# Indirect gathers without a bounds check, with valid row numbers in the empty slots

## The chip, the core and the metric

One core of a Trainium2 chip runs one program: one layer of a graph network over 50,000 nodes and 25,000 edges. The metric is the time of one execution on the device in microseconds (us), as the median of several runs. The engines have their own instruction streams and meet at semaphores: TensorE (PE; PEld is its weight load), VectorE (DVE), ScalarE (ACT), GpSimd (POOL) and SyncE (SP), and 16 DMA engines move the data.

## What is computed

```python
h = relu(layernorm(x))                                  # x: 50000 x 128, f32
agg = segment_sum(edge_attr, src, num_segments=50000)   # edge_attr: 25000 x 128, src: random nodes
z = silu(concat([h, agg]) @ W1 + b1) @ W2 + b2          # W1: 256 x 256, W2: 256 x 128
out = x + layernorm(z) * gamma + beta + h
```

The edges come in no order that is of use to the sum: each edge's row has to reach the node that its `src` names.

## The kernel before

The nodes are cut into NB = 49 blocks of BLOCK = 1024 rows, a block into TILES = 8 tiles of 128 nodes: tile t of a block holds nodes 8p + t, p from 0 to 127. A half block (HALF = 4 tiles) is the unit of work; a block's halves are c = 0 and 1. There are NT = 392 tiles.

**First stage, a sort (to about 125 us).** For each tile a table of 128 slots is filled with the edges whose source node lies in the tile. DVE makes one-hot rows, PE counts with them and places two words per slot (`slot_word`): the edge's number and the node inside the tile. A tile has 64 edges on average, so about half of its slots stay empty: word 0 is 0 there. `slot_tables` (DVE) turns the words into two tables, first for the tiles of FIRST_BLOCKS = 3 blocks (24 columns), later, in DVE's step of block 0, for the other 368: `slot_edge`, the row of `edge_attr` for each slot, and `slot_node`, the node in the tile. To an empty slot's values `empty` = 131072 is added, so that its row number lies beyond the end of the table and its node number matches no node. `link` makes DVE wait for the instruction it wraps. If a tile had more edges than slots, `spilled` is 1, and the other branch of POOL (`spill`) is taken; with these inputs it isn't.

**Second stage, the blocks.** For each tile POOL copies one column of `slot_edge` into `gather_rows` (`name_row`, L459) and issues one indirect DMA (`gather`, L471) that brings 128 rows of 512 bytes of `edge_attr` to G, a ring of RING = 3 blocks. The copy for tile t + 1 stands ahead of the gather of tile t. The gather has `bounds_check=limit, oob_is_err=False`: a row number over the limit moves nothing, G keeps what it held (G is zeroed once at the start). POOL runs two blocks ahead of PE at most: it waits until the edge sum three blocks back is done (`agg_done`).

PE's order for a half: `turn_h` (L636, transposes of the normalised rows), `sum_edges` (L643: waits for the four gathers (`gathered`) and for the one-hot tiles HOT, made by DVE from `slot_node` (L902), then multiplies G by HOT; an empty slot has a zero row in HOT, so whatever finite number lies in G counts for nothing), `layer1` (L654 to L659) and `layer2` of the half before (L667, L671). ACT casts the results to `hi` (L541, L543), DVE takes the rest as `lo` (L911), ACT applies Silu, squares and Relu; DVE does the statistics (`powers`), the scaling and the sums. SP loads X four blocks ahead (L332) and stores the results (L339). Every engine has its loop over blocks written by `run_blocks`: a few blocks in straight code, then a loop of six blocks a turn, and the rest in straight code.

POOL also makes the constants at the start: iotas (`own_node` at L392), zeroed G, then signals `late_const`, which DVE and PE wait for after the sort.

Of the kernel before, what the change touches and what calls it, by code (L numbers as in the profile page):

```python
# [15 lines left out]
P = 128  # L16
# [106 lines left out]
def gnn_layer(nc, x, src, edge_attr, W1, b1, W2, b2, gamma, beta, out):  # L123
# [13 lines left out]
    assert EC % UNROLL == 0 and UNROLL % STREAMS == 0 and NT <= 512  # L137

    HEAD = 2

    GROUP = max(n for n in range(1, 129) if edges % n == 0)

    with ExitStack() as ctx:
        def sb(name, shape, dt):
            return ctx.enter_context(nc.sbuf_tensor(name, shape, dt))
# [50 lines left out]
        edge_f = sb("edge_f", [P, NT], F32)  # L196
        empty = sb("empty", [P, NT], F32)
        own_part = sb("own_part", [P, NT], F32)
        slot_edge = sb("slot_edge", [P, NT], U32)
        slot_node = sb("slot_node", [P, NT], F32)  # L200
        spilled = sb("spilled", [P, 1], F32)
# [163 lines left out]
        def _(pool):  # L365
# [24 lines left out]
            nc.gpsimd.iota(iota_node[:], [[1, P]], base=0, channel_multiplier=0, **small_iota)  # L390
            nc.gpsimd.iota(own_slot[:], [[1, 1]], base=0, channel_multiplier=1, **small_iota)
            nc.gpsimd.iota(own_node[:], [[BLOCK, NB], [1, TILES]], base=0, channel_multiplier=TILES, **small_iota)  # L392
            for j in range(RING):
                done = nc.gpsimd.memset(G[j][:], 0.0)
            done.then_inc(late_const, 1)
# [63 lines left out]
                nc.gpsimd.tensor_copy(gather_rows[b.xj][:, t:t + 1],  # L459
                                      slot_edge[:, bass.ds(b.number(TILES, t), 1)]).then_inc(row_named, 1)  # L460

            def gather(b, c, source, limit):

                at_least(pool, agg_done, b.half(0, 1, 2 - 2 * RING), apart=pool_passed)
                for t in range(c * HALF, (c + 1) * HALF):
                    if t + 1 < TILES:
                        name_row(b, t + 1)
                    elif b.plus(1).exists(NB):
                        name_row(b.plus(1), 0)
                    at_least(pool, row_named, b.number(TILES, t + 1), apart=pool_passed)  # L470
                    nc.gpsimd.indirect_dma_start(  # L471
                        G[b.j][:, t, :], None, source,
                        bass.IndirectOffsetOnAxis(ap=gather_rows[b.xj][:, t:t + 1], axis=0),
                        bounds_check=limit, oob_is_err=False).then_inc(gathered[b.j][c], 16)

            def gather_all(source, last):

                limit = pool.to_reg(last)
                for n in range(2):
                    for c in range(2):  # L480
                        gather(Block(n), c, source, limit)

                def step(b):
                    if b.plus(2).exists(NB):
                        for c in range(2):
                            gather(b.plus(2), c, source, limit)

                run_blocks(pool, step, head=3)

# [1 line left out]
            pool.wait_ge(slots_ready, 1)  # L491
            name_row(Block(0), 0)
            with pool.If(flag != 0):
                gather_all(spill, NB * BLOCK - 1)
            with pool.If(flag == 0):
                gather_all(edge_attr, edges - 1)


        @block.scalar
# [197 lines left out]
        def _(dve):  # L697
            steps = [0]

            def link(instruction):  # L700

                steps[0] += 1
                instruction.then_inc(dve_step, 1)
                dve.wait_ge(dve_step, steps[0])
# [159 lines left out]
            def slot_tables(lo, hi):  # L864

                at = slice(lo, hi)
                nc.vector.tensor_copy(w2i[:, at], slot_word[1][:, at])
                nc.vector.tensor_scalar(out=own_part[:, at], in0=own_node[:, at], scalar1=spilled[:], scalar2=None,
                                        op0=ALU.mult)
                nc.vector.tensor_scalar(out=empty[:, at], in0=slot_word[0][:, at], scalar1=0.0,  # L870
                                        scalar2=float(1 << 17), op0=ALU.is_equal, op1=ALU.mult)
                link(nc.vector.tensor_scalar(out=edge16[:, at], in0=slot_word[0][:, at], scalar1=-1.0, scalar2=16.0,
                                             op0=ALU.add, op1=ALU.mult))
                nc.vector.tensor_scalar(out=w2hi[:, at], in0=w2i[:, at], scalar1=7, scalar2=None, op0=shr,
                                        op1=ALU.bypass)
                link(nc.vector.tensor_scalar(out=w2lo[:, at], in0=w2i[:, at], scalar1=P - 1, scalar2=None, op0=band,
                                             op1=ALU.bypass))
                nc.vector.tensor_tensor(out=edge_f[:, at], in0=edge16[:, at], in1=w2hi[:, at], op=ALU.add)
                link(nc.vector.tensor_tensor(out=slot_node[:, at], in0=empty[:, at], in1=w2lo[:, at], op=ALU.add))
                link(nc.vector.tensor_tensor(out=edge_f[:, at], in0=edge_f[:, at], in1=empty[:, at], op=ALU.add))  # L880
                nc.vector.tensor_scalar(out=slot_node[:, at], in0=slot_node[:, at], scalar1=kept[:],
                                        scalar2=own_slot[:], op0=ALU.mult, op1=ALU.add)
                nc.vector.scalar_tensor_tensor(out=slot_edge[:, at], in0=edge_f[:, at], scalar=kept[:],  # L883
                                               in1=own_part[:, at], op0=ALU.mult, op1=ALU.add).then_inc(slots_ready, 1)
# [112 lines left out]
```

## Time and profile before

| | |
|---|---|
| median of 3 runs | 835.01 us (830.93 to 836.53) |
| the profiled execution | 833.45 us, of which the span from first to last instruction is 831.8 us |
| granted TensorE clock, mean | 0.957 |
| PE, DVE, POOL busy | 88%, 88%, 74% of the span |
| 392 gathers, POOL | 450.1 us, mean 1148 ns |
| 392 copies of row numbers, POOL | 145.9 us |

The profile was taken from one execution. Times in it are in us from the start of the span, durations of one instruction in ns where that is said. In a row of the timeline stand the start, the duration, the engine, the line, the operation, what it writes and reads, and in brackets how long the engine had been idle before it and what ended that. "DMA G<-..." there means that the last thing awaited was a gather's landing; "issue" that the profile shows nothing that was waited for; "remote" that the releaser is not known.

### The profile page before, as it was taken

How to read it: one execution, taken by the hardware profiler on the slowest of the kernel's cores; microseconds unless marked ns; L12 is line 12 of the kernel's file. 1: busy time of each engine (PE TensorE's matmuls, PEld its weight loads, DVE VectorE, ACT ScalarE, POOL GpSimd, SP SyncE). 2: the span in 40 equal slices, each digit the busy share in tenths (PEclk: the TensorE clock that was granted, in tenths of full speed). 3: DMA queues.
4: the chain of work that ended last, by engine and by line, in shares of the span. 5: the costliest groups of instructions: out<-in, count | busy, mean ns of one | idle time of the engine just before them, and what ended most of it. 6: DMA issues, size and time to landing. Idle time of an engine off the chain costs nothing.

```text
span 831.8 us, 19347 instructions
## 1 busy us (share of the span) xinstructions
PE 734.6 (88%) x4567; PEld 602.0 (72%) x4616; DVE 734.0 (88%) x2494; ACT 585.6 (70%) x1927; POOL 617.9 (74%) x831
## 2 busy tenths in 40 slices
PE   4999973899899678998999899989988998989990
PEld 2455542788787657887888788878877887878880
DVE  6999994799996748998999899989888999997995
ACT  4999972687675636787687777868567877776861
POOL 4500006899888887999999989999898899898920
PEclk9999995999999988999999999999999999999996
DMA  5000000123232222332323223232323233231211
GB/s 185 2 0 0 0 0 18 47 71 111 84 122 73 71 73 69 120 121 70 119 76 115 94 93 121 87 103 93 98 73 118 83 107 122 72 102 60 69 58 46
DMA packets 28138, 65.49 MB, mean 79 GB/s; under 512 B 8379, under 2 KB 9934, under 8 KB 28070
## 3 DMA queue, kind: packets, MB, share of 16 engines
q1 hardware_dynamic: 15526, 51.90, 17.5%
q0 software_dynamic: 12544, 12.93, 6.9%
q14 instruction: 54, 0.44, 0.2%
q8 instruction: 14, 0.23, 0.1%
HBM read 51.98 MB, written 25.60 MB: 93 GB/s over the span
## 4 chain that ended last, share of the span: by engine, by line
POOL 35%; issue 26%; PE 25%; DVE 5%; ACT 3%; another core or an unknown queue 2%; DMA 2%; POOLq 1%; DVEq 0%; ACTq 0%; SPq 0%
POOL G L471 22%; POOL gather_rows L459 13%; PE y L671 4%; PE y L613 3%; PE za L643 3%; PE pre L654 2%; PE pre L655 2%; PE pre L659 2%; PE za L608 2%; PE pre L608 2%; PE pre L601 2%; PE za L636 1%; PE za L601 1%; DMA G<-in_edge_attr_dram,gather_rows 1%
## 5 line engine op out<-in xcount | busy, mean ns | idle before, releaser
L471 POOL DMA_INDIRECT G<-in_edge_attr_dram,gather_rows x392 | 450.1, 1148 | 69.1 <-POOL gather_rows L459 41.2
L459 POOL COPY gather_rows<-slot_edge 128x1 uint32 (+1 forms) x392 | 145.9, 372 | 98.4 <-DVE slot_edge L883 91.7
L671 PE MATMUL y<-w2c,S 128*128 128x128 f32 x1568 | 194.2, 276 | 6.5 <-issue 3.2
L671 PEld LDWEIGHTS y<-w2c,S 128*128 128x128 f32 x1568 | 192.9, 193 | 7.8 <-issue 5.3
L911 DVE TENSOR_TENSOR lo<-za,hi 128x1024 fp32r<-128x1024 f32 x98 | 119.7, 1221 | 72.5 <-ACT hi L543 37.8
L534 ACT ACTIVATE H<-X,shift,rstd 128x128 f32<-128x128 f32 x392 | 162.3, 505 | 22.7 <-DVE shift L793 22.7
L654 PE MATMUL pre<-hi,w1h 128*128 128x512 f32 x392 | 168.0, 429 | 0.7 <-issue 0.7
L655 PE MATMUL pre<-hi,w1l 128*128 128x512 f32 x392 | 158.8, 405 | 0.3
L541 ACT CAST hi<-za 128x512 fp32r<-128x512 f32 x98 | 57.5, 587 | 118.0 <-remote 55.0
L549 ACT ACTIVATE S<-pre,b1c 128x512 f32<-128x512 f32 x196 | 125.7, 693 | 9.2 <-remote 4.9
L659 PE MATMUL pre<-lo,w1h 128*128 128x512 f32 x392 | 125.9, 402 | 0.7 <-issue 0.7
L643 PE MATMUL za<-HOT,G 128*128 128x128 f32 x784 | 110.5, 286 | 17.8 <-DMA G<-in_edge_attr_dram,gather_rows 16.6
L643 PEld LDWEIGHTS za<-HOT,G 128*128 128x128 f32 x784 | 100.1, 200 | 20.8 <-DMA G<-in_edge_attr_dram,gather_rows 19.3
L738 DVE BATCH_NORM_STATS2 stat<-X 128x6 f32<-128x128 f32 x392 | 108.6, 283 | 0.0
L556 ACT ACTIVATE junk_sq<-y 128x128 bf16<-128x128 f32 x392 | 103.5, 287 | 3.5 <-PE y L671 3.5
L927 DVE SCALAR_TENSOR_TENSOR T<-y,rstd,gammas 128x128 f32<-128x128 f32 x392 | 105.6, 341 | 0.0
L543 ACT CAST hi<-za 128x512 fp32r<-128x512 f32 x98 | 57.6, 588 | 58.6 <-PE za L643 41.8
L636 PE MATMUL za<-ident,H 128*128 128x128 f32 x392 | 61.7, 281 | 37.3 <-ACT H L534 17.5
L659 PEld LDWEIGHTS pre<-lo,w1h 128*128 128x128 f32 x392 | 75.5, 193 | 19.3 <-issue 0.8
L654 PEld LDWEIGHTS pre<-hi,w1h 128*128 128x128 f32 x392 | 77.3, 197 | 15.0 <-issue 0.9
L655 PEld LDWEIGHTS pre<-hi,w1l 128*128 128x128 f32 x392 | 76.9, 196 | 15.4 <-issue 1.4
L556 ACT ACTIVATION_READ_ACCUMULATOR junk_sq<-y 128x1 f32 x392 | 85.5, 218 | 0.0
(123 smaller groups left out, 1042.2 us busy)
## 6 DMA issues: line engine op xcount, KB each, us to landing
X<-in_x_dram SPq DMA_DIRECT2D x48, 512.0 KB
out_dram<-R SPq DMA_DIRECT2D x48, 512.0 KB
G<-in_edge_attr_dram,gather_rows POOLq DMA_INDIRECT x392
X<-in_x_dram SPq DMA_DIRECT2D x1, 424.0 KB
out_dram<-R SPq DMA_DIRECT2D x2, 212.0 KB
w1f<-in_L_gnn_W_dram SPq DMA_DIRECT2D x1, 256.0 KB, 3.5
w2f<-in_L_gnn_W_dram SPq DMA_DIRECT2D x1, 128.0 KB, 2.7
srci<-in_src_dram SPq DMA_DIRECT2D x1, 97.2 KB
```

Of the source, the lines that this page charges most:

```text
L459: nc.gpsimd.tensor_copy(gather_rows[b.xj][:, t:t + 1], slot_edge[:, bass.ds(b.number(TILES, t), 1)]).then_inc(row_named, 1)
L471: nc.gpsimd.indirect_dma_start(G[b.j][:, t, :], None, source, bass.IndirectOffsetOnAxis(ap=gather_rows[b.xj][:, t:t + 1], axis=0), bounds_ ...
L534: done = nc.scalar.activation(H0[b.j][:, t, :], X[b.xj][:, t, :], ACT.Relu, bias=shift[b.j][:, t:t + 1], scale=rstd[b.j][:, t:t + 1])
L549: nc.scalar.activation(S[c][:, m, :], pre[m][:], ACT.Silu, bias=b1c[:, m:m + 1]).then_inc(silu_done, 1)
L556: done = nc.scalar.activation(junk_sq[:, p, c * HALF + t, :], y[2 * p + c][:, t * D:(t + 1) * D], ACT.Square, scale=float(D) ** -0.5, accu ...
L643: done = nc.tensor.matmul(za[:, 1, t * P:(t + 1) * P], G[b.j][:, c * HALF + t, :], HOT[b.j][:, c * HALF + t, :], start=True, stop=True)
L654: nc.tensor.matmul(pre[m][:], w1h[:, k, cols], hi[c][:, k, :], start=(k == 0), stop=False)
L655: nc.tensor.matmul(pre[m][:], w1l[:, k, cols], hi[c][:, k, :], start=False, stop=False)
L659: done = nc.tensor.matmul(pre[m][:], w1h[:, k, cols], lo[c][:, k, :], start=False, stop=(k == 1))
L671: done = nc.tensor.matmul(place[:, t * D:(t + 1) * D], S[c][:, m, t * P:(t + 1) * P], w2c[:, m, :], start=False, stop=(t == HALF - 1 and m ...
L738: done = nc.vector.bn_stats(stats[b.ring(2)][:, t, :], X[b.xj][:, t, :])
L911: nc.vector.tensor_tensor(out=lo[c][:], in0=za[:], in1=hi[c][:].bitcast(F32), op=ALU.subtract).then_inc(lo_done, 1)
```

## The change

Empty slots get a row number that is in the table. A new constant `spare` (an iota over 392 columns on POOL) holds for partition p, block b and tile t the number 16 + 4p + t + 510b. In `slot_tables` one more DVE instruction, `spare_part`, keeps it where word 0 is 0 and zero elsewhere, and the sum for the row number takes `spare_part` in the place of `empty`. (For an empty slot the rest of the sum is -16, so the rows lie between 0 and 24,995.) `slot_node` still takes `empty`, so HOT is as before. The gathers lose `bounds_check` and `oob_is_err`, and the register with the limit goes.

```diff
+    SPARE_STEP = min(4 * P, (edges - 4 * P - TILES) // (NB - 1))
...
+        spare = sb("spare", [P, NT], F32)
+        spare_part = sb("spare_part", [P, NT], F32)
...
             nc.gpsimd.iota(own_node[:], [[BLOCK, NB], [1, TILES]], base=0, channel_multiplier=TILES, **small_iota)
+            nc.gpsimd.iota(spare[:], [[SPARE_STEP, NB], [1, TILES]], base=16, channel_multiplier=4, **small_iota)
...
                     nc.gpsimd.indirect_dma_start(
                         G[b.j][:, t, :], None, source,
-                        bass.IndirectOffsetOnAxis(ap=gather_rows[b.xj][:, t:t + 1], axis=0),
-                        bounds_check=limit, oob_is_err=False).then_inc(gathered[b.j][c], 16)
-
-            def gather_all(source, last):
-
-                limit = pool.to_reg(last)
+                        bass.IndirectOffsetOnAxis(ap=gather_rows[b.xj][:, t:t + 1], axis=0)).then_inc(gathered[b.j][c], 16)
+
+            def gather_all(source):
...
                 nc.vector.tensor_scalar(out=empty[:, at], in0=slot_word[0][:, at], scalar1=0.0,
                                         scalar2=float(1 << 17), op0=ALU.is_equal, op1=ALU.mult)
+                nc.vector.scalar_tensor_tensor(out=spare_part[:, at], in0=slot_word[0][:, at], scalar=0.0,
+                                               in1=spare[:, at], op0=ALU.is_equal, op1=ALU.mult)
...
                 link(nc.vector.tensor_tensor(out=slot_node[:, at], in0=empty[:, at], in1=w2lo[:, at], op=ALU.add))
-                link(nc.vector.tensor_tensor(out=edge_f[:, at], in0=edge_f[:, at], in1=empty[:, at], op=ALU.add))
+                link(nc.vector.tensor_tensor(out=edge_f[:, at], in0=edge_f[:, at], in1=spare_part[:, at], op=ALU.add))
```

## Rows read from the trace of the kernel before

**Rows 1.** The page: busy shares of the engines, and the chain that ended last.
```profile
PE 734.6 (88%) x4567; PEld 602.0 (72%) x4616; DVE 734.0 (88%) x2494; ACT 585.6 (70%) x1927; POOL 617.9 (74%) x831
...
POOL 35%; issue 26%; PE 25%; DVE 5%; ACT 3%; another core or an unknown queue 2%; DMA 2%; POOLq 1%; DVEq 0%; ACTq 0%; SPq 0%
```

**Rows 2.** Waits, whole span: who waited for whom: us, times, longest.
```profile
POOL gather_rows L459 <- DVE slot_edge L883: 91.7, 1, 91.7
ACT hi L541 <- remote: 55.0, 16, 9.5
...
POOL G L471 <- POOL gather_rows L459: 41.2, 253, 0.6
...
PE za L643 <- DMA G<-in_edge_attr_dram,gather_rows: 16.6, 10, 5.2
...
POOL b2r L408 <- DVE w2sum L839: 9.6, 1, 9.6
```

**Rows 3.** L471's own row, and POOL's timeline at the full ring.
```profile
L471 POOL DMA_INDIRECT G<-in_edge_attr_dram,gather_rows x392: 1023/1028/2734, 130.6 to 795.3; - x196
...
310.62 0.18 POOL L459 COPY gather_rows<-slot_edge 128x1 uint32 x1 [1.26 <-remote]
311.40 1.02 POOL L471 DMA_INDIRECT G<-in_edge_attr_dram,gather_rows  x1 [0.60 <-POOL gather_rows L459]
...
314.45 1.04 POOL L471 DMA_INDIRECT G<-in_edge_attr_dram,gather_rows  x1 [1.45 <-issue]
```

**Rows 4.** The page's group of gathers; POOL's timeline, two undisturbed rows.
```profile
L471 POOL DMA_INDIRECT G<-in_edge_attr_dram,gather_rows x392 | 450.1, 1148 | 69.1 <-POOL gather_rows L459 41.2
...
144.68 0.19 POOL L459 COPY gather_rows<-slot_edge 128x1 uint32<-128x1 uint32 x1
145.03 1.03 POOL L471 DMA_INDIRECT G<-in_edge_attr_dram,gather_rows  x1 [0.16 <-issue]
```

**Rows 5.** PE's timeline: edge sums, undisturbed (five, first and last), and the last.
```profile
354.75 1.06 PE L643 MATMUL za<-HOT,G 128*128 128x128 f32 x8
...
379.33 1.06 PE L643 MATMUL za<-HOT,G 128*128 128x128 f32 x8
...
800.36 1.06 PE L643 MATMUL za<-HOT,G 128*128 128x128 f32 x8
```

**Rows 6.** PE's timeline: edge sums that waited for a gather.
```profile
137.55 2.07 PE L643 MATMUL za<-HOT,G 128*128 128x128 f32 x8 [5.18 <-DMA G<-in_edge_attr_dram,gather_rows]
143.04 1.23 PE L643 MATMUL za<-HOT,G 128*128 128x128 f32 x4 [0.31 <-DMA G<-in_edge_attr_dram,gather_rows]
148.97 1.16 PE L643 MATMUL za<-HOT,G 128*128 128x128 f32 x8 [0.33 <-DMA G<-in_edge_attr_dram,gather_rows]
196.47 1.16 PE L643 MATMUL za<-HOT,G 128*128 128x128 f32 x8 [0.98 <-DMA G<-in_edge_attr_dram,gather_rows]
209.95 1.16 PE L643 MATMUL za<-HOT,G 128*128 128x128 f32 x8 [0.92 <-DMA G<-in_edge_attr_dram,gather_rows]
250.24 1.16 PE L643 MATMUL za<-HOT,G 128*128 128x128 f32 x8 [1.70 <-DMA G<-in_edge_attr_dram,gather_rows]
584.25 1.16 PE L643 MATMUL za<-HOT,G 128*128 128x128 f32 x8 [0.67 <-DMA G<-in_edge_attr_dram,gather_rows]
597.22 1.16 PE L643 MATMUL za<-HOT,G 128*128 128x128 f32 x8 [0.41 <-DMA G<-in_edge_attr_dram,gather_rows]
693.93 1.16 PE L643 MATMUL za<-HOT,G 128*128 128x128 f32 x8 [1.99 <-DMA G<-in_edge_attr_dram,gather_rows]
749.51 1.86 PE L643 MATMUL za<-HOT,G 128*128 128x128 f32 x8 [4.09 <-DMA G<-in_edge_attr_dram,gather_rows]
```

**Rows 7.** Busy us by stretch behind the two longest, granted clock, DMA share, GB/s.
```profile
694.00:701.70 7.70, 7.70 (x41) 6.54 (x42) 7.57 (x20) 4.41 (x15) 6.87 (x10) 0.78 0.11 25
...
749.50:757.30 7.80, 7.79 (x41) 6.83 (x42) 5.28 (x13) 4.37 (x15) 7.00 (x10) 0.78 0.18 56
757.30:763.50 6.20, 6.13 (x43) 5.44 (x43) 4.87 (x25) 4.89 (x16) 5.53 (x9) 1.00 0.28 101
```

**Rows 8.** PE's timeline, the first pass of the loop.
```profile
303.21 0.35 PE L671 MATMUL y<-w2c,S 128*128 128x128 f32 x1 [0.46 <-issue]
```

**Rows 9.** DMA queues: packets, MB, share of 16 engines.
```profile
q1 hardware_dynamic: 15526, 51.90, 17.5%
q0 software_dynamic: 12544, 12.93, 6.9%
```

**Rows 10.** SP's timeline: the last X load; queue 1 from 743 to 744.25 us.
```profile
742.79 0.28 SPq L332 DMA_DIRECT2D X<-in_x_dram  x1
...
q1 hardware_dynamic: 123, 0.50, 103.3%
```

**Rows 11.** DVE's timeline, both slot tables; POOL's iota: busy us, mean ns.
```profile
123.59 0.17 DVE L870 TENSOR_SCALAR empty<-y 128x24 f32<-128x24 f32 x1
123.69 0.17 DVE L872 TENSOR_SCALAR edge<-y 128x24 f32<-128x24 f32 x1
...
148.29 0.53 DVE L870 TENSOR_SCALAR empty<-y 128x368 f32<-128x368 f32 x1
148.74 0.53 DVE L872 TENSOR_SCALAR edge<-y 128x368 f32<-128x368 f32 x1
...
152.48 1.22 DVE L911 TENSOR_TENSOR lo<-za,hi 128x1024 fp32r<-128x1024 f32 x1
...
L392 POOL IOTA own_node<- 128x392 f32 x1 | 0.7, 691 | 0.0
```

More of the change, by code:

```diff
@@ L460, in name_row, with gather @@
                                       slot_edge[:, bass.ds(b.number(TILES, t), 1)]).then_inc(row_named, 1)
-            def gather(b, c, source, limit):
+            def gather(b, c, source):
                 at_least(pool, agg_done, b.half(0, 1, 2 - 2 * RING), apart=pool_passed)
@@ L472, in gather @@
                         G[b.j][:, t, :], None, source,
-                        bass.IndirectOffsetOnAxis(ap=gather_rows[b.xj][:, t:t + 1], axis=0),
-                        bounds_check=limit, oob_is_err=False).then_inc(gathered[b.j][c], 16)
-            def gather_all(source, last):
-                limit = pool.to_reg(last)
+                        bass.IndirectOffsetOnAxis(ap=gather_rows[b.xj][:, t:t + 1], axis=0)).then_inc(gathered[b.j][c], 16)
+            def gather_all(source):
                 for n in range(2):
                     for c in range(2):
-                        gather(Block(n), c, source, limit)
+                        gather(Block(n), c, source)
                 def step(b):
@@ L485, in step @@
                         for c in range(2):
-                            gather(b.plus(2), c, source, limit)
+                            gather(b.plus(2), c, source)
                 run_blocks(pool, step, head=3)
@@ L493, in _ @@
             with pool.If(flag != 0):
-                gather_all(spill, NB * BLOCK - 1)
+                gather_all(spill)
             with pool.If(flag == 0):
-                gather_all(edge_attr, edges - 1)
+                gather_all(edge_attr)
         @block.scalar
```

## The prediction

> **What bounds the kernel now.** I read the page first: busy shares, and the chain that ended last [rows 1]. No engine stands out (PE and DVE 88%, POOL 74%), but POOL's 74% is an average over 125 us in which it had next to nothing to do: its first copy of row numbers waits 91.7 us for the sorted table [rows 2], and POOL is 35% of the chain. So after the sort the kernel has two candidates, POOL (which issues the 392 gathers) and PE (which uses them).
>
> The waits come next [rows 2]. POOL's idle time from then on is almost all its own step from copy to gather (41.2 us, 253 times, 0.6 us at most). It is stopped by a full ring of buffers only once, around 308 to 314 us, for 1.26 + 0.60 + 1.45 = 3.3 us [rows 3]. Otherwise POOL runs at its own pace: a gather 1.03 us, a copy 0.20, a gap 0.16 [rows 4]. With the longer ones, 392 gathers take 450.1 us, 392 copies 145.9 and the gaps 69.1: 665 us from 125.3 to 797.1 us.
>
> PE works in 98 half blocks; each begins its edge sum with one L643 group. Where nothing disturbs it, four of them take 379.33 - 354.75 = 24.58 us, 6.15 each [rows 5]. From the second (143.04) to the last (800.36 [rows 5]) are 96 steps, 590 us at that pace, and it took 657. Of the 67 us lost, the waits for a gather after the first group are 0.31, 0.33, 0.98, 0.92, 1.70, 0.67, 0.41, 1.99 and 4.09, 11.4 us in all [rows 6]. Behind the two longest the granted clock averages 0.78 (part of the stretch at the lower of its two levels, 1.2 GHz), and that half takes 7.70 and 7.80 us against 6.20 for the one behind it: about 1.6 us more each [rows 7]. The rest is not the gathers: in 301 to 306 us PE waits for nothing the profile shows between single matmuls ("issue") [rows 8], and ACT, DVE and "remote" waits in the loop [rows 2]. PE and POOL are thus nearly even: mean steps of 6.8 us for either. A POOL that is faster takes the gather waits away and then meets PE's own pace; a POOL that is slower becomes the bound at once.
>
> **The change, part by part.**
>
> *Gather issue (L471).* The same 392 instructions, without the check. No row of before has a gather without one, so the price is open. The duration is 1023 ns at least and 1028 at the median [rows 3]; the number of filled slots of a tile (from the inputs: 42 to 97 of 128, 64 on average) varies widely beside a duration that hardly does. So a skipped row is not cheaper on POOL than a fetched one, and doubling the fetched rows should cost POOL nothing. What dropping a compare and a select from each of 128 rows gives lies between 0 and, at the far end, 1.03 - 0.20 = 0.83 us (a POOL instruction over 128 x 1 numbers, the copy [rows 4]). It is one operation of several a row needs (index, address, two ends of the transfer), so I take a tenth, 0.1 us, 39 us of POOL's time. That is a choice, not a reading. Upward I allow 0.05 us (the gathers of 1.03 to 1.04 leave no room for more without another path).
>
> What PE gets back saturates. Up to the wait at 250.24 the waits sum to 0.31 + 0.33 + 0.98 + 0.92 + 1.70 = 4.24 us, over the first 72 gathers: 0.06 us a gather removes them. Behind the full ring at 314 us [rows 3] the four late waits sum to 7.16 us over 245 gathers: 0.03 us a gather removes them. With 0.1 us all nine go: -11.4 us; the two clock dips behind 1.99 and 4.09 go with them: 2 x 1.6 = -3.2; the first wait (5.18 [rows 6]) shrinks by four gathers: -0.4. The other 28 us of POOL's saving go into waiting for agg_done, as at 310 us.
>
> *The transfers.* An empty slot now brings 512 bytes. Queue 0 moved 12.93 MB in 6.9% of 16 engines' span [rows 9]; 392 x 128 x 512 bytes are 25.7 MB. At queue 1's rate (51.90 MB in 17.5%, 45 us an MB) the 12.8 MB more are 572 us, 0.09 us of each of 16 engines per gather; if queue 0's time doubles instead (918 us), 0.15 us. Against a gather every 1.7 us there is room: 24% of DMA time becomes 29 to 31%. A landing is thus 0.1 us later, and more where it meets an X load: the first 1.25 us behind the last X load's issue (742.79) move X alone and fill the engines, and the 4.09 wait follows it [rows 6, 10]. In a run of halves that follow POOL that is paid once, not every time. I charge it once at the first gather, 0.1 us, if POOL gets ahead, and at about ten waits, 1 to 2 us, if it doesn't.
>
> *DVE.* One more instruction per slot table. In the first (24 columns) it issues about 0.1 us behind the `empty` one (123.59 to 123.69), ahead of POOL's first copy [rows 11]: +0.1 us on the path. In the second (368 columns) 0.45 us (148.29 to 148.74), where DVE is without a gap and the next lo, 152.48, comes later by that: +0.45. The add at L880 changes only its operand. *POOL:* one more iota over 392 columns, 0.69 us [rows 11], before 20 us, where POOL then waits 9.6 us for w2sum [rows 2], so hidden by that; without it 0.7 us in a stretch that has 91.7 us of room. The limit register written once goes: nothing.
>
> *Sum, against the profiled span of 831.8 us:* -11.4 - 3.2 - 0.4 + 0.1 + 0.1 + 0.45 = -14.4. Its run took 833.45, the median of the runs is 835.01. Median: 835.0 - 14.4 = 820.6; I round to 821.
>
> **The rivals.**
> *The check was free (0.31).* The issue stays 1.03 us. For it: the constant duration, which also fits 128 rows treated alike by something that isn't limited by arithmetic on indices. Against: only that work is taken out. Then +0.1 + 0.45 + 1 to 2 us of later landings: 837 (835 to 839).
> By the Trainium skill ("DMA: Bandwidth & Descriptors", the anatomy of one DMA on the SWDGE path) generating the descriptors is a small, variable part of a transfer issued from GpSimd, and many can be emitted before their number shows; work saved per row would then be saved nowhere, which is this rival's result. The constant 1.03 agrees as far as it goes, but all gathers here have 128 rows, so no row shows what fewer would cost.
> *A little is saved (0.10),* 0.01 to 0.05 us a gather: the late waits go first, -7.2 - 3.2 + 0.65 = about -10 at 0.03 us, the early ones half: 823 to 832.
> *The issue becomes longer (0.12).* POOL is the bound already over long stretches, so a longer issue is paid 392 times less the 3.3 us of ring wait. At +0.03 us: 392 x 0.03 - 3.3 = +8.5, 843.5, from which point on it is slower by over 1%; at +0.05 us +16, 851. For it: nothing in the rows, except that the mean, 1148 ns [rows 4], lies above the median, 1028, from a cause that isn't shown. Against: less work per row, and the number of rows fetched leaves the duration alone.
> *My forecast (0.47):* 0.06 us a gather or more. 815 (all 16.6 us of gather waits and the dips gone) to 826 (another wait takes the place of a third).
>
> **How the numbers follow.** About 1% (8.3 us) can be told from no change. Faster by over 1% (under 826.7): 0.46 of my case and 0.02 of the little saved, 0.48. Slower by over 1% (over 843.4): 0.10 of the third rival, and 0.02 for landings that cost more than priced, 0.12. Within 1%: 0.40. The range 815 to 840 takes in my case, the free check and the little saving and leaves out the longer issue and the tails.
>
> **What would show it.** L471's median under 0.97 us (right), at 1.02 to 1.03 (the check was free), over (rival three). If right: waits of PE L643 on the gathers fall from 16.6 us to about 5, nearly all of it the first; POOL shows waits for PE ("remote", "issue") of 20 us or more; PE's steps of 6.15 stay, as do the "issue" stalls of 301 us. In every case queue 0 moves 25.8 MB in 11 to 14% of the engines' span. I am wrong if the issue doesn't move, or if it falls and ACT, DVE or "issue" waits in front of L636 grow by what the gather waits lose.

## Result: slower by 2%, and the profile after

| kernel | time, us | ratio to before, 95% interval |
|---|---|---|
| before | 834.88 (830.93 to 836.53) | |
| after | 853.54 (849.25 to 864.16) | 1.0213 (1.0139 to 1.0288) |

The ratios, here and below, leave out every execution that took over 1.5% more than the fastest of its kernel.

The profiled execution took 849.25 us; its span is 847.7 us, 15.9 more than before's 831.8. The line numbers of after are shifted: the gather is L475 (was L471), its copy L463, the edge sum L645 (was L643), the lo subtraction L915.

The page of after: busy times, the queue of the gathers, the chain by engine, the group of gathers.
```profile
PE 736.3 (87%) x4567; PEld 603.5 (71%) x4616; DVE 735.3 (87%) x2496; ACT 584.2 (69%) x1927; POOL 589.7 (70%) x832
...
q0 software_dynamic: 12544, 25.72, 11.7%
...
PE 44%; ACT 15%; DVE 15%; issue 13%; another core or an unknown queue 9%; POOL 1%; DMA 1%; DVEq 1%; ACTq 0%; SPq 0%; POOLq 0%
...
L475 POOL DMA_INDIRECT G<-in_edge_attr_dram,gather_rows x392 | 409.8, 1045 | 72.6 <-POOL gather_rows L463 38.4
```
The waits of after, whole span, and the gathers' own row.
```profile
DVE lo L915 <- issue: 47.6, 11, 13.2
ACT hi L545 <- remote: 39.9, 19, 7.9
POOL gather_rows L463 <- PE za L645: 22.4, 15, 3.6
PE za L645 <- DMA G<-in_edge_attr_dram,gather_rows: 5.1, 2, 4.9
...
L475 POOL DMA_INDIRECT G<-in_edge_attr_dram,gather_rows x392: 944/976/1540, 131.6 to 795.7; - x196
```
POOL did what was forecast: busy for 589.7 us, where it was for 617.9 [rows 1]. A gather takes 0.976 us at the median where it took 1.028 [rows 3], 1.045 on the mean where it took 1.148 [rows 4]. POOL went from 35% of the chain to 1% [rows 1]. PE's waits for gathers fell from 16.6 us to 5.1 [rows 2, 6], nearly all of it the first. Yet PE's way from its first edge sum to its last took 677.9 us, 15.1 more than the 662.8 of before.

Where the time went is seen in the starts of the edge sums. PE's timeline after, the first seven half blocks (four lines of the fourth left out):
```profile
149.81 1.06 PE L645 MATMUL za<-HOT,G 128*128 128x128 f32 x8
171.72 0.37 PE L645 MATMUL za<-HOT,G 128*128 128x128 f32 x1 [0.95 <-issue]
...
184.90 1.06 PE L645 MATMUL za<-HOT,G 128*128 128x128 f32 x8
191.03 1.06 PE L645 MATMUL za<-HOT,G 128*128 128x128 f32 x8
197.16 1.06 PE L645 MATMUL za<-HOT,G 128*128 128x128 f32 x8
```
The kernel before, run again (e12 below), the same sums:
```profile
149.71 1.16 PE L643 MATMUL za<-HOT,G 128*128 128x128 f32 x8
155.95 1.16 PE L643 MATMUL za<-HOT,G 128*128 128x128 f32 x8
163.24 1.16 PE L643 MATMUL za<-HOT,G 128*128 128x128 f32 x8 [0.67 <-DMA G<-in_edge_attr_dram,gather_rows]
169.59 1.16 PE L643 MATMUL za<-HOT,G 128*128 128x128 f32 x8
176.41 1.16 PE L643 MATMUL za<-HOT,G 128*128 128x128 f32 x8 [0.43 <-DMA G<-in_edge_attr_dram,gather_rows]
```
From the third sum to the seventh are four steps, 24.6 us at PE's pace of 6.15 [rows 5]. After needs 197.16 - 149.81 = 47.35, 22.8 too many; before needs 26.70, 2.1 too many (3.3 in its first profile). I call this the **early loss**. All other steps together lose 58.6 us in after and 63.0 in before. So the loss in four steps is larger than the whole difference.

In this stretch PE is mostly idle, and the profile names little that it waits for. After, by stretch (busy us and instructions of PE, PEld, DVE, ACT, POOL; granted clock; DMA share; GB/s):
```profile
150.00:154.00 4.00, 2.49 (x14) 1.72 (x12) 3.86 (x10) 0.69 (x1) 3.52 (x7) 1.00 0.19 47
154.00:158.00 4.00, 1.22 (x4) 1.01 (x5) 0.83 (x2) 0.69 (x1) 3.50 (x7) 0.91 0.16 39
158.00:162.00 4.00, 3.35 (x16) 2.88 (x16) 0.00 (x0) 0.58 (x1) 3.52 (x7) 0.66 0.19 49
162.00:166.00 4.00, 1.42 (x4) 0.66 (x3) 0.00 (x0) 0.00 (x0) 3.51 (x7) 0.77 0.18 49
166.00:170.00 4.00, 0.35 (x2) 0.35 (x3) 1.92 (x5) 2.13 (x5) 3.51 (x7) 0.50 0.20 49
...
174.00:178.00 4.00, 1.54 (x5) 1.21 (x6) 2.10 (x6) 0.62 (x2) 0.97 (x1) 0.50 0.15 33
```
In four of these stretches PE takes 2 to 5 matmuls in 4 us, where it takes 19 to 34 in before. The records stand 0.70 us apart, loads of weights and matmuls alike:
```profile
162.50 0.27 PE L673 MATMUL y<-w2c,S 128*128 128x128 f32 x1 [0.90 <-issue]
163.22 0.36 PE L673 MATMUL y<-w2c,S 128*128 128x128 f32 x1 [0.45 <-issue]
163.92 0.42 PE L673 MATMUL y<-w2c,S 128*128 128x128 f32 x1 [0.35 <-issue]
```
This is the form of stall that before has at 301 to 306 us [rows 8], only earlier and longer. The clock is not its beginning: it is at full (1.00) in 150 to 154 us, when PE is already down to 14 matmuls, and still 0.91 in the next 4 us, with 4 of them; it falls to 1.2 GHz (0.50) behind PE's idle time.

PE isn't the first to stand still; ACT is. In after's timeline of PE, then of ACT:
```profile
148.66 0.62 PE L661 MATMUL pre<-lo,w1h 128*128 128x512 f32 x2
...
156.78 0.50 PE L656 MATMUL pre<-hi,w1h 128*128 128x512 f32 x1 [3.28 <-issue]
```
```profile
151.04 0.69 ACT L551 ACTIVATE S<-pre,b1c 128x512 f32<-128x512 f32 x1 [1.79 <-remote]
156.04 0.69 ACT L551 ACTIVATE S<-pre,b1c 128x512 f32<-128x512 f32 x1 [4.31 <-remote]
...
167.47 0.58 ACT L545 CAST hi<-za 128x512 fp32r<-128x512 f32 x1 [7.90 <-remote]
```
The second Silu has its input (`pre`) at 149.28 and by the kernel's text waits for nothing else, yet it starts at 156.04. The cast at 167.47 has its input, the edge sum of 149.81, at 150.87. PE's 3.28 us of "issue" end 0.05 us behind the Silu, whose buffer PE writes next: e2's profile (below) has the same gap and names ACT. DVE's longest wait (13.2 us, lo) ends with ACT's cast. In the kernel before run again, the same Silu is 0.56 us late; and before's own stall at 301 us has the same order: ACT's cast has its input at 297.7 us and starts at 306.2, while PE keeps its pace until about 301. First e2's PE, then ACT of e12 and of before:
```profile
156.87 0.50 PE L657 MATMUL pre<-hi,w1h 128*128 128x512 f32 x1 [3.27 <-ACT S L552]
```
```profile
149.31 0.69 ACT L549 ACTIVATE S<-pre,b1c 128x512 f32<-128x512 f32 x1 [0.56 <-PE pre L659]
```
```profile
306.16 0.59 ACT L541 CAST hi<-za 128x512 fp32r<-128x512 f32 x1 [9.51 <-remote]
```
So the stall takes several engines. This Silu's idle time is 3.6 to 5.1 us in nine of the eleven profiles below and above that have an early loss of 5 us or more (e8 and e17, whose stall comes a step later, have 0.3 and 0.4 there, then 8.5 and 5.3 before a cast) and 0.3 to 1.4 us in the nine without.

One more row goes with it: the queue that loads PE's written-out code moved no packet between 160 and 170 us in after, and one of 16 KB there in before's repeat:
```profile
q8 instruction: 1, 0.02, 0.8%
```

### The profile page after: what moved, and what is told of

It reads as the page before. It is cut to its first block, busy times and chain, and to the rows that moved or that the text cites. A ratio compares the mean times of both kernels' runs of the same rounds, so it can differ in the third digit from the quotient of the medians.

```text
span 847.7 us, 19349 instructions
## 1 busy us (share of the span) xinstructions
PE 736.3 (87%) x4567; PEld 603.5 (71%) x4616; DVE 735.3 (87%) x2496; ACT 584.2 (69%) x1927; POOL 589.7 (70%) x832
## 3 DMA queue, kind: packets, MB, share of 16 engines
q1 hardware_dynamic: 15526, 51.90, 17.2%
q0 software_dynamic: 12544, 25.72, 11.7%
## 4 chain that ended last, share of the span: by engine, by line
PE 44%; ACT 15%; DVE 15%; issue 13%; another core or an unknown queue 9%; POOL 1%; DMA 1%; DVEq 1%; ACTq 0%; SPq 0%; POOLq 0%
PE y L673 9%; PE za L645 6%; ACT H L536 5%; PE pre L656 5%; PE pre L657 5%; PE pre L661 5%; PE za L638 4%; ACT junk_sq L558 3%; PE y L615 3%; DVE T L931 3%; ACT S L551 3%; DVE lo L915 2%; PE za L610 2%; PE pre L610 2%
## 5 line engine op out<-in xcount | busy, mean ns | idle before, releaser
L475 POOL DMA_INDIRECT G<-in_edge_attr_dram,gather_rows x392 | 409.8, 1045 | 72.6 <-POOL gather_rows L463 38.4
L463 POOL COPY gather_rows<-slot_edge 128x1 uint32 (+1 forms) x392 | 157.2, 401 | 122.3 <-DVE slot_edge L887 91.7
L915 DVE TENSOR_TENSOR lo<-za,hi 128x1024 fp32r<-128x1024 f32 x98 | 119.7, 1222 | 81.4 <-issue 47.6
L536 ACT ACTIVATE H<-X,shift,rstd 128x128 f32<-128x128 f32 x392 | 162.3, 506 | 17.2 <-DVE shift L795 15.9
L551 ACT ACTIVATE S<-pre,b1c 128x512 f32<-128x512 f32 x196 | 125.3, 694 | 22.1 <-remote 19.4
L645 PE MATMUL za<-HOT,G 128*128 128x128 f32 x784 | 111.6, 287 | 11.3 <-issue 6.2
L645 PEld LDWEIGHTS za<-HOT,G 128*128 128x128 f32 x784 | 101.6, 201 | 13.3 <-issue 7.3
L638 PE MATMUL za<-ident,H 128*128 128x128 f32 x392 | 63.5, 286 | 54.5 <-ACT H L536 30.7
L638 PEld LDWEIGHTS za<-ident,H 128*128 128x128 f32 x392 | 45.2, 145 | 63.1 <-issue 38.8
```

The costliest lines, as they stand in the source:

```text
L463: nc.gpsimd.tensor_copy(gather_rows[b.xj][:, t:t + 1], slot_edge[:, bass.ds(b.number(TILES, t), 1)]).then_inc(row_named, 1)
L475: nc.gpsimd.indirect_dma_start(G[b.j][:, t, :], None, source, bass.IndirectOffsetOnAxis(ap=gather_rows[b.xj][:, t:t + 1], axis=0)).then_in ...
L536: done = nc.scalar.activation(H0[b.j][:, t, :], X[b.xj][:, t, :], ACT.Relu, bias=shift[b.j][:, t:t + 1], scale=rstd[b.j][:, t:t + 1])
L551: nc.scalar.activation(S[c][:, m, :], pre[m][:], ACT.Silu, bias=b1c[:, m:m + 1]).then_inc(silu_done, 1)
L638: done = nc.tensor.transpose(za[:, 0, t * P:(t + 1) * P], H0[b.j][:, c * HALF + t, :], ident[:])
L645: done = nc.tensor.matmul(za[:, 1, t * P:(t + 1) * P], G[b.j][:, c * HALF + t, :], HOT[b.j][:, c * HALF + t, :], start=True, stop=True)
```

## Experiments

All start from the kernel after unless said otherwise. Step n leads from the start of edge sum n to that of sum n + 1. "Halves 3 and 4" in the expectations are steps 3 and 4.

| run | ratio to before beside it, 95% | early loss, us | other steps, us |
|---|---|---|---|
| e0 after again | 1.0184 (1.0135 to 1.0233) | 19.9 | 58.3 |
| e1 check kept | 0.9994 (0.9968 to 1.002) | 1.1 | 59.2 |
| e2 half rows | 1.0161 (1.0081 to 1.0241) | 22.1 | 57.1 |
| e3 pause | 0.9992 (0.9946 to 1.0038) | 1.5 | 49.8 |
| e6 pause early | 1.0095 (1.0007 to 1.0183) | 19.7 | 60.6 |
| e7 pause later | 1.0009 (0.993 to 1.0088) | 21.9 | 47.8 |
| e8 late once | 1.015 (1.0066 to 1.0234) | 27.2 | 56.2 |
| e9 PE's head | 1.007 (0.9962 to 1.0178) | 22.4 | 63.9 |
| e10 pause not run | 1.0195 (1.0126 to 1.0264) | 22.1 | 50.6 |
| e11 pause run only | 0.9992 (0.9953 to 1.003) | 3.6 | 59.2 |
| e12 before again | 0.999 (0.9956 to 1.0023) | 2.1 | 54.9 |
| e13 pause again | 1.0019 (0.9966 to 1.0072) | 1.6 | 54.8 |
| e14 early long | 1.0276 (1.0195 to 1.0357) | 1.5 | 83.8 |
| e15 two blocks | 1.0304 (1.0191 to 1.0418) | 2.0 | 89.0 |
| e16 all long | 1.0194 (1.0113 to 1.0276) | 1.8 | 80.7 |
| e17 early again | 1.0381 (1.0271 to 1.0491) | 20.3 | 71.0 |
| e18 one ahead | 1.0134 (1.0082 to 1.0187) | 5.0 | 72.3 |
| e19 two ahead | 1.0144 (1.0091 to 1.0196) | 8.0 | 70.7 |

Both losses are starts of edge sums less 6.15 us a step, one profile each. The runs were on four chips, where the kernel before took 824.3 us (e0 to e3), 839.8 (e6 to e9), 825.9 (e10 to e13), and 837.5 and 834.6 (e14 to e17, e18 and e19, one chip). Columns can be compared within such a group. Of the kernel before there are two profiles only, that of the first result and e12's: beside e0 to e3, e6 to e9 and e14 to e19 its early loss isn't known.

**Is it the extra transfer?** e0 repeats after. e1 puts the check back and keeps the valid row numbers, so all 25.7 MB move:
```diff
-                        bass.IndirectOffsetOnAxis(ap=..., axis=0)).then_inc(...)
+                        bass.IndirectOffsetOnAxis(ap=..., axis=0),
+                        bounds_check=limit, oob_is_err=False).then_inc(...)
```
e2 leaves the check out and fetches 256 bytes a row, half of each edge row, and sums only these:
```diff
-                        G[b.j][:, t, :], None, source,
+                        G[b.j][:, t, 0:D // 2], None, source,
...
+                source = source.rearrange("e (h d) -> (e h) d", h=2)
```
e3 leaves the check out and puts one small POOL instruction ahead of each copy:
```diff
+                nc.gpsimd.memset(pause[:, t % 2:t % 2 + 1], 0.0)
                 nc.gpsimd.tensor_copy(gather_rows[b.xj][:, t:t + 1], ...)
```


> The changed kernel itself, again, beside the others on one chip. In its first profile the gather took 976 ns at the median against 1028 before, and the waits of PE for gathers fell from 16.6 to 5.1 us, but PE's 97 steps took 677.9 us against 662.8. Theory A (more transfer: every empty slot moves 512 bytes, queue 0 25.7 MB against 12.9) and theory B (POOL is ahead and runs against the full ring of G) both expect about 853 us here. Theory C (chance: the stalls in which PE's signals come late fall anywhere, and before had few of them) expects a result between the two kernels, under 845.

> The changed kernel with the bounds check put back: every row number is in the table, so it rejects nothing and all 128 rows move. The gather's issue should be back at 1.03 us, queue 0 still at 25.7 MB. Theory A (more transfer) expects it slow, 850 us or more. Theory B (POOL ahead) expects it near the kernel before, 835 to 839 us, with POOL's waits for PE gone and the waits for gathers back at 16 us.

> The changed kernel with gathers of 128 pieces of 256 bytes (the table seen as twice as many rows of 64 numbers) into the left half of each tile of G: the sums over edges are not those of the reference. As many rows per gather and no check, so POOL is as fast as in the changed kernel, but queue 0 moves 12.9 MB as before. Theory A (more transfer) expects the forecast gain: 818 to 825 us. Theory B (POOL ahead of PE) expects 850 us or more.

> The changed kernel with one memset over 128 x 1 numbers in front of each copy of row numbers on POOL, which costs about 0.1 us, as much as the gather lost. Traffic as in the changed kernel, POOL's pace as before. Theory A expects 850 us or more; theory B expects 835 to 840 us.

The transfer is cleared. The groups of gathers and queue 0 of e1, then of e2:
```profile
L475 POOL DMA_INDIRECT G<-in_edge_attr_dram,gather_rows x392 | 448.9, 1145 | 68.3 <-POOL gather_rows L463 42.8 <-issue 25.5
...
q0 software_dynamic: 12544, 25.72, 11.7%
```
```profile
L475 POOL DMA_INDIRECT G<-in_edge_attr_dram,gather_rows x392 | 427.4, 1090 | 69.2 <-POOL gather_rows L463 38.1 <-issue 31.1
...
q0 software_dynamic: 12544, 12.87, 8.1%
```
e1 moves all the bytes and has before's time; e2 moves before's bytes and is as slow as after. The gathers of e3 are as short as after's (977 ns) and it has before's time. So the gather instruction without a check does no harm by itself: the sequence of gathers that has become quicker does.

**POOL's pace, and when?** e6 keeps the pause for the gathers of blocks 0 to 4 (up to about 205 us), e7 for all others; e8 puts one memset of 128x1024 ahead of block 1's gathers; e9 writes nine blocks ahead of PE's loop in place of three.
```diff
+                if b.turn is None and b.n < 5:          # e6; e7: the contrary
+                    nc.gpsimd.memset(pause[:, t % 2:t % 2 + 1], 0.0)
...
+                if b.is_number(1) and c == 0:           # e8
+                    nc.gpsimd.memset(pause[:], 0.0)
...
-            run_blocks(pe, step, head=3)
+            run_blocks(pe, step, head=9)                # e9
```


> The kernel after, with the pause of about 0.1 us ahead of each copy kept only for the gathers of blocks 0 to 4 (20 of the 49 x 4 half-block groups of work come before about 205 us); from block 5 on POOL runs at full speed. Theory E (what costs is the early stretch alone: between 153 and 178 us TensorE takes one instruction per 0.70 us and loses 20 to 23 us, and this comes only when the gathers run at their full speed there): the stall is absent, POOL gets ahead later without harm, and the time is at least as good as with the pause everywhere, 815 to 825 us where the kernel before has 824. Theory L (POOL's lead of 15 to 30 us over TensorE costs all along, by what its gathers do to the others): the lead comes back after block 5, and the time is 833 to 840 us.

> The counterpart: full speed for the gathers of blocks 0 to 4, the pause of 0.1 us ahead of each copy from block 5 on. Theory E: the crawl at 0.70 us per instruction between 153 and 178 us is there, the halves 3 and 4 take 30 to 37 us together in place of 12.3, and the time is 838 to 848 us. Theory L: the lead that the stall gives is used up by the slower POOL, the time is 822 to 830 us.

> The kernel after at full speed everywhere, with one single memset of 128x1024 (0.95 us by the row of the same shape on G) ahead of the gathers of block 1. This separates pace from phase. Theory E-phase (the early stall hangs on POOL being at one exact place when TensorE's code is to be loaded at about 164 us): one delay of 0.95 us is enough, the load is there, and the time is 815 to 828 us. Theory E-pace (it needs a POOL that is slower at each gather): the stall stays, 838 to 848 us. Theory L expects 838 to 848 us too, since POOL comes ahead all the same.

> The kernel after with another layout of TensorE's code only: nine blocks written out ahead of its loop in place of three, and 30 blocks in the loop in place of 36 (the tail keeps its length). The work and its order are the same. Theory E: the crawl in halves 3 and 4 hangs on how TensorE's instructions are fetched, so it moves or goes: either a load of 16 KB at about 164 us and no crawl, 815 to 830 us, or a crawl at another place of the written-out part. Theory L: the time stays at 838 to 848 us, and the halves 3 and 4 take 30 to 37 us together as before.

All four have the early loss. For e7 and e8 that is what "full speed early" predicts: a single delay (e8) only moves the stall on by one step (14.6 and 22.9 us for steps 4 and 5). e9 went against theory E, by which another layout of PE's code should have moved the stall or ended it; it stayed in steps 3 and 4 (34.6 us). e6 went against theory E too: its pauses go on to 186.7 us, past the whole stall, so that POOL runs what it runs in e3, and it stalls. The intervals of e6, e7 and e9 reach to 1.00 or close to it, on a chip where before too was 15 us above e0 to e3's, so the ratios decide little here. e7 has an early loss of 21.9 us and before's time: either before loses time there as well, or the other steps give it back (47.8 us, the least of all).

**The place of POOL's code, or its pace?** e10 writes the pauses only into the branch for spilled edges, which these inputs don't run; e11 only into the branch that runs; e12 is the kernel before, e13 the pause everywhere, once more.
```diff
+                pausing[0] = True                       # e10
                 gather_all(spill)
+                pausing[0] = False
...
+                pausing[0] = True                       # e11
                 gather_all(edge_attr)
```


> The kernel before once more, with a profile of its own, as the control: its first profile shows the halves 3 and 4 of TensorE in 15.5 us and 16 KB of code loaded at 166.5 us. Theory K (the early stall belongs to the kernel's code and comes in each execution of it): the two halves take 12 to 16 us again, the time is that of the runs of before, ratio 1.000 within 0.005. Theory C (the stall comes by chance in any of these kernels, or by chip): the halves may take over 28 us here too, and the profiled time is then some 15 us above the fastest.

> The kernel with the pause of about 0.1 us ahead of each copy everywhere, once more, beside the control on this chip. Theory K: halves 3 and 4 take 12 to 16 us, the time is within 1% of before, as in its first run. Theory C: the stall may come here, and the time is then 10 to 20 us above before.

> The kernel after, with the pauses written only into POOL's branch for spilled edges, which these inputs never run. POOL runs the same instructions at the same pace as after; only its code lies elsewhere, as in the paused kernel. Theory K-place (the place of POOL's code decides whether the early stall comes): no stall, halves 3 and 4 in 12 to 16 us, time 820 to 830 us where before has 824 (or within 1% of before on another chip). Theory K-pace (what POOL does decides): the stall is there, 28 to 38 us for the two halves, and the time is 1.5 to 2.5% above before.

> The counterpart: the pauses only in the branch that runs, none in the branch that doesn't. POOL runs what it ran in the kernel with the pause everywhere, from code that starts where that of after starts. Theory K-place: the stall is there, time 1.5 to 2.5% above before. Theory K-pace: no stall, halves 3 and 4 in 12 to 16 us, and the time within 1% of before.

What POOL runs acts, and not where its code lies. By stretch, e10 and then e11:
```profile
162.00:166.00 4.00, 0.38 (x2) 0.19 (x1) 0.13 (x1) 0.74 (x2) 3.52 (x7) 0.70 0.19 49
```
```profile
162.00:166.00 4.00, 3.66 (x27) 3.03 (x26) 2.42 (x3) 4.00 (x16) 3.55 (x7) 1.00 0.54 180
```
Two matmuls against 27 in the same 4 us. e10 (unchanged stream, code moved) has the loss and the time of after; e11 (the paused stream) has neither. But the ratios of the kernels with the small pause flatter them. Their single times lie in two groups (e3: seven of 820 to 826 us, one at 834, two at 838; e11: seven of 822 to 830, three of 839 to 846) or spread (e13: 821 to 847), while e12's lie in 821 to 828. Over all ten executions e13's median is 833.1 us and e11's 830.0, beside 825.9 for before; e1's is 823.6 beside 824.3. With the small pause the stall seems to come in some executions, which also fits e6. That is read from times alone, since each kernel has one profile. The chip is a second reading that isn't excluded: the three profiles without the stall (e3, e11, e13) are from the two chips where before takes 824 to 826 us, the two with it (e6, e17) from those where it takes 838 to 840.

**What the pace does.** In the kernels without an early loss POOL ends the gathers of a half 1.4 to 6.7 us ahead of its edge sum in these steps, 2 us or less in half of them, and PE waits for some. I call this POOL's lead. (At the third sum it is 1.4 to 2.6 us without an early loss; at the last sum ahead of the stall, the third or in e8 and e17 the fourth, 1.8 to 2.9. It is no sharp bound.) If being held by the gathers keeps the stall away, a longer pause must do so surely, and its end must bring the stall. e14 pauses by a memset of 128x128 (0.2 us) in blocks 0 to 4, e15 in blocks 0 to 2, e16 everywhere; e17 is e6 again.
```diff
+                if b.turn is None and b.n < 5:          # e14; e15: b.n < 3; e16: always
+                    nc.gpsimd.memset(pause[:, t % 2, :], 0.0)
```


> The kernel after with a longer pause, a memset of 128x128 (about 0.2 us), ahead of each copy for blocks 0 to 4 only; full speed from block 5 on. Theory M (TensorE's short waits for the gathers cover the first pass over its written-out code; once POOL's lead in the first halves is over some 2 us TensorE runs without a pause and its code comes late): the lead of POOL in the halves 1 to 6 stays at 1.4 to 1.7 us, no halves over 9 us before 185 us, and the time is 810 to 824 us where before has 825. Theory N (the stall has nothing to do with TensorE waiting for gathers): the stall comes as in the run with the short early pause, 838 to 848 us.

> The same pause of about 0.2 us for the gathers of blocks 0 to 2 only, which POOL issues up to about 180 us. Theory M: no stall in halves 3 and 4; one may come later, up to about 210 us, where TensorE runs code for the first time with POOL ahead. Time 810 to 826 us without one, 835 to 845 us with one. Theory N: the stall in halves 3 and 4, 838 to 848 us.

> The same pause of about 0.2 us ahead of every copy. POOL's cycle is then some 0.1 us longer per gather than with the check, or 0.4 us per half: TensorE is held by the gathers all through with a lead near 1.6 us. Theory M: no stall, and halves of 6.2 to 6.6 us each, 828 to 845 us from the slower gathers alone. Theory N: the stall on top, 845 to 865 us.

> The kernel with the short pause of 0.1 us for blocks 0 to 4 once more, on this chip: its first run was on one where the kernel before took 840 us. In the kernels with that pause everywhere, POOL's lead at half 3 was 1.7 to 2.3 us, near the edge of theory M, and their times fell in two groups, 820 to 831 and 834 to 846 us. Theory M: the runs fall in two such groups here too, 812 to 828 and 834 to 848 us. Theory N gives one group only.

The early loss is gone in all three (1.5, 2.0, 1.8 us), and in e14 and e15 a stall comes once the pause has ended (at 195 and 167 us) and POOL has drawn ahead: e15 takes 30.5 us for step 9, where the lead was 3.7 us, e14 12.6, 9.8 and 14.9 us for steps 16 to 18, from a lead of 4.9 us. e16, whose PE is held all through, has no step over 9.1 us, and pays with 57.9 us of waits for gathers; its 850.5 us are over the 845 expected. So the stall is not tied to the place in the code at 150 to 178 us; in these runs it follows PE getting free of the gathers. A lead alone doesn't bring it: e11, paused all through, has one of 9.8 us by sum 12 and over 25 later, and no step over 9.8. The times that I expected of e14 and e15 (810 to 826) were wrong for that very reason: the stall was put off, not avoided. e17's stall came one step later than e6's, and its four times make one group (860 to 869), not two.

**What ends a stall.** e15 by stretch of 2 us, and POOL's timeline:
```profile
212.00:214.00 2.00, 0.00 (x0) 0.39 (x2) 0.00 (x0) 0.00 (x0) 1.84 (x3) 0.50 0.30 66
...
216.00:218.00 2.00, 0.42 (x2) 0.47 (x2) 0.00 (x0) 0.00 (x0) 0.87 (x1) 0.50 0.24 66
...
220.00:222.00 2.00, 2.00 (x11) 1.86 (x9) 1.58 (x5) 2.00 (x11) 0.00 (x0) 0.50 0.03 8
```
```profile
215.89 0.98 POOL L478 DMA_INDIRECT G<-in_edge_attr_dram,gather_rows  x1 [0.16 <-issue]
226.07 0.81 POOL L466 COPY gather_rows<-slot_edge 128x1 uint32 x1 [9.21 <-PE za L648]
```
POOL's ring is full and it stops at 216.9 us; PE, at one instruction per 0.7 us for 20 us, is back at its pace from 219.2. In after POOL stops at 175.0 us:
```profile
174.06 0.97 POOL L475 DMA_INDIRECT G<-in_edge_attr_dram,gather_rows  x1 [0.16 <-issue]
178.66 0.18 POOL L463 COPY gather_rows<-slot_edge 128x1 uint32<-128x1 uint32 x1 [3.63 <-PE za L645]
```
and PE is back at 177.4. The full ring may end the stall, or only follow from PE's standing still. e18 and e19 make the ring fill sooner: a half's gathers wait until the half two, or three, before it is summed.
```diff
-                at_least(pool, agg_done, b.half(0, 1, 2 - 2 * RING), apart=pool_passed)
+                at_least(pool, agg_done, b.half(c, 1, -1), apart=pool_passed)   # e18; e19: -2
```


> The kernel after, POOL's gathers at full speed, but a half's gathers wait until TensorE has summed the half but one before it, in place of the block three before: POOL can be one half ahead of TensorE, not five. Theory P (once TensorE is behind in loading its code it stays slow for as long as POOL issues gathers without a pause; in the profiles POOL's ring fills 1.5 to 3 us before each slow stretch ends, after a burst of five halves or some 24 us): the burst is one half, about 5.5 us, so a stall costs about 5 us and not 22, the later ones too; the time is 812 to 828 us on a chip where before has 825, within 1% of before or better. Theory Q (POOL's full ring only follows the stall and has no part in its length): the stall of 20 to 24 us is there though POOL stands still, and the time is 1.5 to 2.5% above before.

> The same with one half more: a half's gathers wait for TensorE's sum of the half three before it, POOL can be two halves ahead. Theory P: a stall lasts for the issue of two halves, about 11 us, in place of 22 to 24; the time lies between that of the tighter limit and that of after, within 1.5% of before. Theory Q: as with the tighter limit, 20 to 24 us lost and 1.5 to 2.5% above before.

The length follows the limit: 5.0 us (expected about 5) and 8.0 (expected 11) in place of 22.8. e18, POOL's timeline and the stretch; e19's:
```profile
154.76 0.18 POOL L463 COPY gather_rows<-slot_edge 128x1 uint32<-128x1 uint32 x1 [1.71 <-remote]
...
162.00:166.00 4.00, 4.00 (x24) 3.28 (x23) 3.43 (x8) 4.00 (x15) 3.50 (x6) 1.00 0.52 164
```
```profile
154.00:158.00 4.00, 0.70 (x4) 0.51 (x4) 1.44 (x3) 0.69 (x1) 3.54 (x6) 1.00 0.17 51
158.00:162.00 4.00, 3.75 (x17) 3.29 (x17) 0.34 (x1) 1.54 (x4) 1.92 (x4) 0.57 0.12 33
```
The stall of e19 ends in the stretch in which POOL pauses (1.92 us busy). So the early stall is kept up by POOL's uninterrupted gathers. Shorter ones can end without a pause: in e7, after step 28 (12.3 us), PE is back at its pace by 348 us, with POOL issuing all along. The time, however, did not come back: 1.3% and 1.4% above before, where I had expected within 1% for e18. In e18 the tight limit holds PE at the gathers again (25.9 us of waits for them); in e19 pairs of slow steps (9.7 and 10.8, 9.3 and 11.2, 9.7 and 11.6 us) come where the lead has room to grow from 4 or 5 us to 8 or 14. None of the variants beats before.

## Why the prediction was wrong

*POOL.* Right in direction, half the size: the issue falls by 0.052 us at the median, where I chose 0.1. That is just outside my own case (0.06 or more, a median under 0.97) and beside the small saving (up to 0.05). The mean fell by 0.103, but it varies by 0.057 (1.045 to 1.102) between kernels with one and the same gather. Rivals "free" and "longer" are out: L475's median is 0.976, against 1.02 to 1.03 for the one and above it for the other. The Trainium skill ("DMA: Bandwidth & Descriptors", the anatomy of one DMA on the SWDGE path) calls the generation of descriptors small and variable. My reading of it, that work saved per row would be saved nowhere, isn't in it, and the traces disagree: 1.028 against 0.976 us for 128 rows.

*The transfers, DVE, the iota.* Right: 25.72 MB in 11.7% (said: 25.8 in 11 to 14%), and e1 shows that with the added DVE work and all the bytes the time is before's within 0.3%.

*PE's waits for gathers.* Right as a row, 16.6 to 5.1 us, and POOL now waits for PE (22.4 us and more). Wrong as a gain. The steps outside the early ones lose 58.6 us in after against 63.0 in before's first profile and 54.9 in its second: the 11.4 us booked for the waits and the 3.2 for the dips don't show in them. e1, held by the gathers (21.3 us of waits), loses 59.2 there. What PE no longer waits for the gathers it waits for something else, ahead of the transposes above all, where my closing line had looked for it. Before, then after:
```profile
L636 PE MATMUL za<-ident,H 128*128 128x128 f32 x392 | 61.7, 281 | 37.3 <-ACT H L534 17.5
```
```profile
L638 PE MATMUL za<-ident,H 128*128 128x128 f32 x392 | 63.5, 286 | 54.5 <-ACT H L536 30.7
```
That is 17.2 us more, 13.2 of them for ACT's H, against 11.5 us less for gathers. The saving was counted from one execution and from one engine's waits, and the repeat shows 28.2 us of such waits in a kernel that took 8.5 us less span than the first. A wait that other waits stand behind is no term of a sum.

*"PE's steps of 6.15 stay, as do the issue stalls of 301 us."* This is the step that failed. I had seen the stall [rows 8], taken it as fixed and put its growth at nothing, without a reason. "The first pass of the loop" over these rows is wrong as well: PE's loop takes blocks 3 to 8 in its first turn, and the stall lies in the step of block 11, in the second, with no packet on the queue of PE's code from 250 to 600 us. The stall can come earlier and last longer: where POOL runs ahead it comes in the very first steps, at 22.8 us, and 22.8 - 3.3 = 19.5 us is more than the result; the other steps give back 63.0 - 58.6 = 4.4, which leaves the 15.1. In before it came at step 24, once POOL's lead had grown from 3 to 12 us (a step of 17.0 us). A row at hand pointed to it: the full ring at 310 us [rows 3] stood right behind the stall at 303 us, the same pair as in after. My closing line named ACT, DVE or "issue" waits growing as the way to be wrong, but only by what the gather waits lose, and with no chance and no price; 0.12 for slower was too small.

*What stays open.* Why ACT starts late on inputs that are there and PE's instructions come 0.7 us apart while POOL issues gathers without a pause, and why this rarely begins while PE is held by them. Late code and late signals between engines are both possible. That PE's code isn't there is inferred: from "issue" with nothing awaited, from one pace for all kinds of instruction, and from the code load at 160 to 170 us that is in the profiles of before, e1, e3, e11 to e16 and e18 and not in after, e0, e2, e6, e7, e9 and e10 (e8 and e19 have it 10 us later; e17, whose stall came later, has it). Against it as the whole cause stand ACT's idle time, which comes first, and stalls with no such load near: before's at 301 us, and e2's step 55 (22.9 us, 516 to 538 us), in the fifth turn of PE's loop, with no packet on that queue from 510 to 560 us. Whether slow loading is a cause or a companion was not tried.

## What to carry over

When a change frees an engine that others wait for, don't book its waits as gain before knowing what runs in their shadow: here a stall of several engines could grow there, and freeing POOL by 5% of a gather cost 2% of the kernel. Price the "issue" stalls of a profile as something that can move and grow, and look at whether the supplier's buffers are full just behind each. Ask of a wait marked "issue" or "remote" what the kernel's text makes that instruction wait for, and when that was done: it shows which engine stood still first. And where an added load and a quicker instruction come in one change, a run that undoes one of the two (e1, e2) tells which of them acts.

## What the runs showed of the hardware

- An indirect gather of 128 rows of 512 bytes issues in 0.976 us at the median without the check (up to 0.982 in e16) and 1.028 with it (1.032 in e12); rows of 256 bytes don't shorten it (0.976). Its mean (1.045 to 1.102 without, 1.145 and 1.148 with) varies more between profiles than the check is worth.
- The early stall, in which ScalarE starts late on inputs that are there (up to 7.9 us idle in after) and TensorE takes one instruction per 0.70 us, lasted about as long as GpSimd went on issuing gathers: it cost 19.7 to 27.2 us with a ring of five halves ahead, 8.0 with two, 5.0 with one. The granted clock falls to 1.2 GHz only after it has begun.
- A pause of about 0.1 us per gather, one memset of 128x1 (114 ns in its row), kept it away in three profiles of three (e3, e11, e13), though single times of these kernels reach 838 to 847 us; the same pause for the first five blocks only did not, in two of two (e6, e17), on other chips.
